# A four-layer gated cross-attention and expert network: the last batch's reciprocal sums are spread by TensorE instead of through memory

## The reference

```
b, n, m = 8, 256, 256;  HEADS = 8;  DIM_HEAD = 64
q = (layer_norm(x) @ Wq)            # 8 heads of 64
k, v = split(layer_norm(context) @ Wkv)
sim  = einsum('bhid,bhjd->bhij', q, k) * DIM_HEAD ** -0.5
attn = softmax(sim)                 # over j
out  = einsum('bhij,bhjd->bhid', attn, v)
out  = out.reshape(b, n, 512) @ Wout + bout
x    = x + tanh(g_xattn[1]) * out
```

## Time and profile before

| | |
|---|---|
| median of three executions | 1940.14 us |
| span of the profiled execution | 1940.0 us |
| TensorE busy | 92% |
| VectorE busy | 57% |
| ScalarE busy | 39% |
| GpSimd busy | 13% |
| mean granted TensorE clock | 0.963 of full speed |

### The profile page before, as it was taken

One profiled execution on the slowest core, in us unless ns is written; L12 is line 12 of the kernel. 1 busy time (PEld: TensorE's weight loads), 2 busy tenths in 40 slices (PEclk: granted clock), 3 DMA queues, 4 the chain that ended last, 5 costly groups with the idle time before them and its releaser, 6 DMA issues. The chain is left out here.

```text
span 1940.0 us, 28231 instructions
## 1 busy us (share of the span) xinstructions
PE 1792.1 (92%) x9401; PEld 1282.2 (66%) x9401; DVE 1111.1 (57%) x3199; ACT 750.1 (39%) x1727; POOL 259.1 (13%) x277
## 2 busy tenths in 40 slices
PE   6999899889999799999978699999989999999789
PEld 4666565656666556888857568888655666656475
DVE  4888786656777653222237674111446777776666
ACT  5566654346546411111126322222124444445331
POOL 2000301121102210000041330000040001000114
PEclk9999898999999999999989799999989999999899
DMA  7562303221102233454444478333322111111363
GB/s 237 154 209 94 116 1 107 70 79 28 38 24 55 88 109 105 153 167 162 151 130 146 168 269 288 128 117 130 111 69 71 46 47 34 36 31 42 102 190 109
DMA packets 171310, 213.99 MB, mean 110 GB/s; under 512 B 17177, under 2 KB 137634, under 8 KB 171042
## 3 DMA queue, kind: packets, MB, share of 16 engines
q1 hardware_dynamic: 160114, 184.63, 29.8%
q0 software_dynamic: 10496, 27.28, 4.4%
q10 hardware_dynamic: 560, 0.27, 0.0%
HBM read 149.99 MB, written 57.93 MB: 107 GB/s over the span
## 5 line engine op out<-in xcount | busy, mean ns | idle before, releaser
L1293 PE MATMUL a_s<-a_kT,a_qT 32*128 32x256 f32 (+2 forms) x1024 | 186.9, 473 | 19.4 <-ACT a_probs L1450 9.8
L1309 PEld LDWEIGHTS a_t<-kept_ident,a_probs 128*128 128x128 f32 x1280 | 142.5, 145 | 88.5 <-issue 49.4
L1309 PE MATMUL a_t<-kept_ident,a_probs 128*128 128x128 f32 x1280 | 182.9, 287 | 5.3 <-DVE a_probsT L1698 1.6
L1326 PE MATMUL a_o_bank<-a_probsT,a_v 128*64 128x256 f32 (+1 forms) x1280 | 170.7, 397 | 13.8 <-ACT a_o_raw L1480 9.7
L1698 DVE COPY a_probsT<-a_t 128x512 f32<-128x512 f32 x266 | 170.3, 680 | 0.8 <-PE a_t L1309 0.6
L758 POOL DMA_INDIRECT slots_in<-f_xn,f_slot x88 | 85.1, 968 | 473.3 <-DVE f_slot L535 449.5
L2862 PE MATMUL r_bank<-r_w,r_hT 128*128 x624 | 139.3, 379 | 1.0 <-DVE r_hT L3006 1.0
L1444 ACT ACTIVATE a_probs<-a_s,a_negmax 128x512 f32<-128x512 f32 x128 | 86.9, 683 | 136.6 <-DVE a_negmax L1680 136.4
L1293 PEld LDWEIGHTS a_s<-a_kT,a_qT 32*128 32x128 f32 (+1 forms) x1024 | 88.9, 189 | 75.7 <-issue 37.2
L2862 PEld LDWEIGHTS r_bank<-r_w,r_hT 128*128 128x128 f32 x624 | 118.4, 190 | 22.8 <-issue 7.5
L1454 ACT ACTIVATE a_probs<-a_s,a_negmax 128x256 f32<-128x256 f32 x256 | 102.1, 472 | 80.8 <-DVE a_negmax L1684 80.5
(11 more groups left out here) (398 smaller groups left out, 3145.4 us busy)
## 6 DMA issues: line engine op xcount, KB each, us to landing
r_firsts<-in_f_w SPq DMA_DIRECT2D x27, 1024.0 KB, 5.3
r_firsts<-in_f_w SPq DMA_DIRECT2D x46, 512.0 KB, 4.4
slots_in<-a_zeros SPq DMA_DIRECT2D x8, 2048.0 KB, 13.1
half_in<-a_zeros SPq DMA_DIRECT2D x8, 1024.0 KB, 9.5
a_share_of<-shares_out SPq DMA_DIRECT2D x32, 256.0 KB, 3.9
r_w<-in_f_w SPq DMA_DIRECT2D x8, 1024.0 KB, 6.0
r_xg<-slots_in SPq DMA_DIRECT2D x28, 256.0 KB, 3.0
slots_out<-r_y SPq DMA_DIRECT2D x28, 256.0 KB, 2.2
```

The lines of the kernel that those rows point to most:

```text
L1293: last = nc.tensor.matmul(out, qT[rows, e % 2, m, c, t * P:(t + 1) * P], kT[rows, e % 2, c, :], start=True, stop=True)
L1309: last = nc.tensor.transpose(bank[:, n * P:(n + 1) * P], src, ident[:, :])
L1326: last = nc.tensor.matmul(o_bank[g * R:(g + 1) * R, 0:SEQ], v[:, e % 2, kt, h, :], probsT[:, half, i, kt, :], start=(kt == 0), stop=(kt == ...
```

## The change

For the last batch (e = 7) of layers 1 and 3 alone, `finish_jobs` puts other jobs in the places of `sums` and `share`. VectorE takes the reciprocal of `sums` as it lies (128 x 16). TensorE then multiplies, at the step of `share`: with the reciprocals' column `inverse[:, g, at]` repeated over 64 columns as the weights and the identity as the moving matrix, a product writes 64 rows that all hold the 128 reciprocals. There are 16 such products of 128 columns, eight in each of two PSUM banks. VectorE multiplies two blocks of `o_raw` by each bank. SyncE leaves the last batch out. Batches 0 to 6 are as before.

```diff
--- before.py
+++ after.py
@@ -860,8 +860,15 @@
     def finish_jobs(b, u):
         jobs = []
         for kind, t, later, at in cfg.finish:
-            if at == u and 0 <= b - later < BATCH:
-                jobs.append((kind, b - later, t))
+            e = b - later
+            if at != u or not 0 <= e < BATCH:
+                continue
+            if e == BATCH - 1 and kind == "sums":
+                jobs.append(("inverse", e, t))
+            elif e == BATCH - 1 and kind == "share":
+                jobs += [("spread", e, 0), ("spread", e, 1)]
+            else:
+                jobs.append((kind, e, t))
         return jobs
 
     SUMS_AT = next((later * NU + at for kind, _, later, at in cfg.finish if kind == "sums"), 0)
@@ -933,7 +940,7 @@
             t_at["pT", bb, (uu, 0)] = len(t_at)
             t_at["pT", bb, (uu, 1)] = len(t_at)
         for kind, e, n in prep_jobs(b, u) + finish_jobs(b, u):
-            if kind != "share":
+            if kind not in ("share", "inverse"):
                 number(kind, e, n)
         for kind, e, n in extra[s]:
             if kind in ("f_turn", "f_logits", "f_count"):
@@ -975,6 +982,7 @@
         exp_table = sb("exp_table", [P, 1])
         rsums = sb("rsums", [P, TB, H]) if PACK > 1 else None
         sums = sb("sums", [P, 2, GROUPS * BLOCKS * TB]) if PACK == 1 else None
+        inverse = sb("inverse", [P, GROUPS, BLOCKS * TB]) if PACK == 1 else None
         o_raw = sb("o_raw", [P, 2, BLOCKS, SEQ])
         o = sb("o", [P, TB, VW]) if PACK > 1 else None
         if cfg.project:
@@ -1023,6 +1031,7 @@
         shares_stored = sem("shares_stored") if cfg.project else None
         shares_in = sem("shares_in") if cfg.project else None
         shared_out = sem("shared_out") if cfg.project else None
+        inverted = sem("inverted") if cfg.project else None
         rope_split = sem("rope_split") if cfg.rope else None
         rope_moved = [sem(f"rope_moved{j}") for j in range(NC_ // 2)] if cfg.rope else None
         rope_done = sem("rope_done") if cfg.rope else None
@@ -1093,7 +1102,7 @@
 
             def spread_shares(until):
 
-                while cfg.project and spread[0] < BATCH and spread[0] * NU + SUMS_AT < until:
+                while cfg.project and spread[0] < BATCH - 1 and spread[0] * NU + SUMS_AT < until:
                     e, spread[0] = spread[0], spread[0] + 1
                     if e > 0:
                         sp.wait_ge(shares_in, 16 * GROUPS * e)
@@ -1342,9 +1351,22 @@
                 bank = t_turn(t_at["sums", e, 0])
                 nc.tensor.transpose(bank[0:GROUPS * BLOCKS * TB, 0:P], sums[:, e % 2, :], ident[:, :]).then_inc(t_full, 1)
 
+            def spread_inverse(e, j):
+                bank = t_turn(t_at["spread", e, j])
+                pe.wait_ge(inverted, 1)
+                for i in range(2 * TB):
+                    at = 2 * j * TB + i
+                    for g in range(GROUPS):
+                        last = nc.tensor.matmul(bank[g * R:(g + 1) * R, i * P:(i + 1) * P],
+                                                inverse[:, g, at:at + 1].to_broadcast([P, R]), ident[:, :], start=True, stop=True)
+                last.then_inc(t_full, 1)
+
             def project_out(e, t):
                 n = t_at["y", e, t]
-                pe.wait_ge(shared_out, e + 1)
+                if e < BATCH - 1:
+                    pe.wait_ge(shared_out, e + 1)
+                else:
+                    taken(pe, t_at["spread", e, 1])
                 bank = t_turn(n)
                 for c in range(OC):
                     last = nc.tensor.matmul(bank[:, 0:D], o_raw[:, e % 2, c, t * P:(t + 1) * P], wo[:, c, :],
@@ -1374,6 +1396,8 @@
                         turn_back(e, t)
                     elif kind == "sums":
                         turn_sums(e)
+                    elif kind == "spread":
+                        spread_inverse(e, t)
                     elif kind == "y":
                         project_out(e, t)
                 for kind, e, n in extra[s]:
@@ -1630,6 +1654,17 @@
                 dve.wait_ge(shares_in, 16 * GROUPS * (e + 1))
                 nc.vector.tensor_tensor(o_raw[:, e % 2, :, :], o_raw[:, e % 2, :, :], share_of[:, :, :], ALU.mult
                                         ).then_inc(shared_out, 1)
+
+            def invert_sums(e):
+                dve.wait_ge(s_free, s_at["qk", e, (NU - 1, 1)] + 1)
+                nc.vector.reciprocal(inverse[:, :, :].rearrange("p g n -> p (g n)"), sums[:, e % 2, :]).then_inc(inverted, 1)
+
+            def share_spread(e, j):
+                n = t_at["spread", e, j]
+                dve.wait_ge(t_full, n + 1)
+                dve.wait_ge(o_free, (e + 1) * BLOCKS)
+                heads = o_raw[:, e % 2, 2 * j:2 * j + 2, :]
+                nc.vector.tensor_tensor(heads, heads, t_bank(n)[:, :].rearrange("p (c n) -> p c n", c=2), ALU.mult).then_inc(t_free, 1)
 
             def move_y(e, t):
                 n = t_at["y", e, t]
@@ -1707,6 +1742,10 @@
                         move_sums(e)
                     elif kind == "share":
                         share(e)
+                    elif kind == "inverse":
+                        invert_sums(e)
+                    elif kind == "spread":
+                        share_spread(e, t)
                     else:
                         move_y(e, t)
                 if cfg.mask and u == 0 and b + 1 < BATCH:
```

## The result

The changed kernel takes 1921.33 us (median of 4 runs, 1919.23 to 1922.16), the kernel before on the same chip 1938.28 (4 runs, 1935.99 to 1943.54): ratio 0.9913 [0.9895, 0.9931].

What follows compares the result with a forecast made beforehand. TensorE, busy 92% of the span, was taken as the bound, so its pauses at both attention ends hold the kernel up. Savings of 6.2 + 4.9 + 1.0 = 12.1 us from 1940.0 gave 1927.9, stated as 1928.0, range 1922 to 1937.

Steps and rivals of the forecast that it cites:

- The spread products overlap: On TensorE, the new products run on alternating array halves like the product with the values, 1.2 us per bank.
- S: Time of one bank's spread products on TensorE, taken as 1.2 us at full clock, twice that at half clock.
- Rival C: Both layers' ends: spread products don't overlap and run at half clock, so the kernel gets slower, 1943 to 1958; chance 0.05.
- Layer 1, 6.2 us: Layer 1's attention end: output products start 3.6 us earlier and run at full clock, saving 2.56 us more.
- Chain: Stretch from the end of the last product with the values to the output products, forecast as 2S + 0.8 = 3.2 us.
- Layer 3, 4.9 us: Layer 3's attention end: the next stage's first product starts at 1839.2 instead of 1844.11.
- rival A: Layer 3's end: the clock isn't kept, S is 2.4 and nothing is won there; time 1934, chance 0.18.
- SyncE's loads first, VectorE late next: Layer 3's border: SyncE's 18 loads, moved earlier, end at 1837.4, so VectorE's last row at 1838.15 ends the block.
- The clock after it, 1.0 us: Stages behind both attentions: less time at half clock saves 1.0 us in layer 3 and nothing in layer 1.
- rival D: More than forecast: both next stages start at full clock, 14.8 us, and S = 1.08 adds 0.5; time 1925, chance 0.08.
- rival B: Behind layer 1's attention: gain given back as the clock falls at other places; time 1931 to 1936, chance 0.09.
- The base: Starting time of the sum: profiled span 1940.0, within 0.2 us of the runs' median 1940.14.

Runs made afterwards that it cites:

- e2: The changed kernel run again without alteration; ratio 0.9910 [0.9885, 0.9935] to the kernel before.
- e9: The changed kernel run a third time without alteration; ratio 0.9916 [0.9895, 0.9938] to the kernel before.
- e6: Changed kernel, but in layer 3 SyncE holds its 18 loads until the last product with the values is done; ratio 0.9984 to the kernel before, slower chip.
- e10: Changed kernel, with the last 6 of layer 3's 18 SyncE loads issued in the next stage instead of ahead of the border; ratio 0.9938 to the kernel before.
- e5: Kernel before, with nine unused TensorE products of 256 columns filling the last batch's pause; ratio 0.9994 to the kernel before, slower chip.
- e1: The kernel before run again without alteration, for a second profile; ratio 0.9997 [0.9984, 1.0011] to its first measurement.

## Why the prediction was right or wrong

By its own steps, with what the profile after (and e2) measured:

- **The spread products overlap**, right. S was 0.98 us in layer 1, both banks 1.95, where 1.2 each was taken; 0.061 us per record, below the lower bound of 0.0675 from half of a 256-column record. So what the prediction took for a bound was none.
  The rule that the prediction quotes from the Trainium skill ("TensorE: Matmul & The Clock Gate", Part 3, Packing small matmuls) would have S = 2.6 by its estimate; the trace doesn't agree with it, and going by the rows was right. Rival C is out: no run was slower.
- **Layer 1, 6.2 us**: 6.8. Chain 2.53 us instead of 3.2; output products 3.72, as said. The smaller S, and the first spread product's start 0.19 us ahead of the end of the product with the values, make up the 0.6.
- **Layer 3, 4.9 us**: 4.4. "The clock had just come back when the spread begins" did not hold: it was so only in the execution from which it was read. In the profile after the clock was back only within 1820-1821, some 5.5 us after the product with the values began, where before it was 3.3, and the first bank went at half clock (chain 3.48 us, not 3.2). That is rival A's condition; but it came back in time for the output products (3.72), so A's price was hardly paid: that was luck and not forecast. In e9 it was back sooner, and the chain took 2.62.
- **SyncE's loads first, VectorE late next**, right: e6 puts them back and loses 4.9 us, e10 takes them away and wins nothing. The margin is 0.6 us in the profile after, 0.1 in e2, and in e9 it was SyncE that ended last.
- **The clock after it, 1.0 us**: this is the step that failed, a term of the sum that was sized too small. It measured 3.8 in the profile after: 1.7 in layer 1, where nothing was taken, and 2.1 in layer 3, where 1.0 was. That was rival D, held at 0.08. For layer 1's nothing the prediction gives no reason; nearest to one is its word under rival B that the pauses at the borders are fixed by the program. But the pause alone doesn't decide: in layer 1 it is 1.54 us before and after, and the clock was at 0.51 in one and 1.00 in the other. What differs is what TensorE did ahead of the pause: in the earlier trace rows it stood still for 5.67 us and came back from half clock at 679-680; now it had been at work almost without a break since before the product with the values. Filling the pause alone did the same in its one profile (e5, 7.10 us). The clock is still lost here at times: it was lost in three of three profiles in which TensorE stood still in the chain, and in three of ten with the change. So the change moved the odds and not a fixed price, as far as thirteen profiles can tell. By these counts it is worth an estimated 1.2 us here (0.7 of 1.7), and what decides between the executions of one program is not shown.
- **The base.** The three runs had their median at 1940.14; 4 runs had it at 1938.28, 21 runs on another occasion at 1937.08. The highest of the runs shown was 7.5 us above the lowest, so a median of three was worth some 2 us, and I took it for the time.

The 6.7 us between 1928.0 and 1921.33 are then: 2.9 from the terms (15.0 at the two ends instead of 12.1), 1.9 from the base (1940.14 to 1938.28), and 1.9 from the rest, of which the stretch from 981 to 1120, 1.5 us, is seen and not explained. Over three comparisons the gain was 17.0, 15.8 and 15.2 us by the medians (e2's against 1937.08, e9's against 1938.16). The range's lower end had D with 3 us for the scatter of the runs; with the base's own doubt it should have gone to 1919 (1922 less some 3).

## What to carry to other kernels

Where TensorE stands still for 5 us in front of a stage's end, count three prices: the wait, the half clock of the work behind it, and the half clock behind the next pause; in layer 1 they were 4.3, 2.6 and, in seven profiles of ten, 1.7 us. Before the gain of a shorter chain is booked, look at every queue that runs into the same border, and see what a moved instruction was queued ahead of: layer 3 gained nothing without SyncE's new order (e6), and a load that came to stand behind six others cost some 6 us (e10). And take the scatter of the time before into the range as well as that of the time after.

## What the hardware showed that was not expected

- The clock's return is not a fixed time after work begins. In layer 3 it came 3.3 us after the last product with the values began in the profile before, some 5.5 us after it in the profile after. With the same program, the 16 records of that product took 3.55 and 3.31 us (before, e1), and the spread behind it 2.94, 2.82 and 2.09 us (after, e2, e9).
- A float32 product whose weights are one column repeated costs no more than another: 0.058 to 0.061 us per record of 128 columns over half the array, where the product with the values has 0.135 for 256.
- The reciprocal of 128 x 16 from SBUF takes 0.24 us, that of 16 x 128 from PSUM 0.95, for the same 2048 numbers. Which of the two differences counts, the shape or the memory, no run tells.
- One chip ran the kernel before in 2020 us, the others in 1937 to 1939. Parts of the program took the same time on it (layer 3's border 17.49 us in e5 as in before, VectorE's end 11.89 in e6 against 11.93), others longer: the stretch from 981 to 1120 was 24 to 25 us longer in e5 than in before. What slows them is not shown.
